# Gate, best and sums for two groups at once, and the chain of scales behind its statistics, in a fused two-layer metaformer kernel

## The reference, cut to what matters

```python
# x: (4, 128, 128, 128) = batch, channels, height, width
x = x + deform_conv(_ln_c(x), w_off, w_conv)             # layer 0, conv
t = _to_tokens(x)                                        # (4, 16384, 128)
t = t + moe(_ln_t(t), router_w, router_b, expert_w, expert_b)   # 8 experts, the best 2 of each token
x = _from_tokens(t, x)
x = x + fourier_conv(_ln_c(x), alphas, betas)            # layer 1, conv: real part is a channel mix and a reversal of the pixels
t = _to_tokens(x)
t = t + soft_moe(_ln_t(t), gate_w, gate_b, weight1, weight2)

def soft_moe(x, ...):                                    # the part that the change touches most
    logits = einsum('bsd,ed->bse', x, gate_w) + gate_b   # 64 experts
    probs = softmax(logits, axis=1)                      # over the 16384 tokens of an image
    vals, idx = top_k(probs.transpose(0, 2, 1), 8)       # the 8 best tokens of each expert
    # gather those tokens, weigh them, two-layer network with gelu, scatter back
```

## Time and profile before

| | before |
|---|---|
| median of 3 runs | 3716.45 us (3716.29 to 3724.53) |
| profiled execution | 3721.06 us |
| span of its instructions | 3719.3 us |
| PE, DVE busy | 3471.8 us (93%), 2835.3 us (76%) |
| ACT, POOL busy | 1759.2 us (47%), 2049.9 us (55%) |
| DVE's wait for `P` (L1231) | 8.2 us in all |
| steady part of `phase_bc` | two steps in 21.9 us |

### The profile page before, as it was taken

The page is one execution under the profiler, slowest core; times in us unless marked ns, Lnnn a source line. Parts: engine busy times, 40 slices in busy tenths (PEclk is TensorE's granted clock), DMA queues, the critical chain, the costliest instruction groups (busy, mean ns, idle before and its releaser), DMA issues. The chain is left out here.

```text
span 3719.3 us, 89516 instructions
## 1 busy us (share of the span) xinstructions
PE 3471.8 (93%) x30679; PEld 2278.8 (61%) x30679; DVE 2835.3 (76%) x8858; ACT 1759.2 (47%) x5333; POOL 2049.9 (55%) x3060
## 2 busy tenths in 40 slices
PE   5999999999999999999987999999999999995668
PEld 4776777777777776777754555555555555553445
DVE  4777777777777767777637999999999999996534
ACT  3444444444444444444411555555555555555234
POOL 4666656666566665666524556665566556654210
PEclk7999999999999999999988999999999999997855
DMA  5555555555555555555526887888788878884689
GB/s 117 130 125 133 125 119 129 125 133 126 118 129 125 132 126 117 126 127 122 113 66 236 295 301 278 292 297 300 280 289 301 295 285 289 312 319 163 241 338 395
DMA packets 665753, 750.30 MB, mean 202 GB/s; under 512 B 104801, under 2 KB 531937, under 8 KB 648914
## 3 DMA queue, kind: packets, MB, share of 16 engines
q1 hardware_dynamic: 559826, 670.61, 58.1%
q10 hardware_dynamic: 104448, 71.85, 6.4%
q0 software_dynamic: 1024, 2.10, 0.2%
HBM read 552.36 MB, written 181.50 MB: 197 GB/s over the span
## 5 line engine op out<-in xcount | busy, mean ns | idle before, releaser
L421 PE MATMUL a_sb<-a_sr,wcv 128*128 128x512 f32 (+3 forms) x2820 | 1052.0, 515 | 0.8 <-DVE a_xo L557 0.8
L403 PEld LDWEIGHTS a_sb<-a_tt,a_win 32*128 32x128 f32 x19008 | 642.9, 187 | 124.2 <-issue 124.0
L421 PEld LDWEIGHTS a_sb<-a_sr,wcv 128*128 128x128 f32 x2820 | 492.9, 190 | 335.0 <-issue 289.9
L403 PE MATMUL a_sb<-a_tt,a_win 32*128 32x144 f32 (+1 forms) x19008 | 661.8, 292 | 25.8 <-ACT a_yr L462 7.4
L1231 DVE TENSOR_TENSOR b_P<-b_P,b_x 128x1024 f32<-128x1024 f32 x512 | 604.1, 1210 | 8.4 <-DMA b_P<-pd 8.2
L480 ACT COPY a_sr<-a_sb 128x432 f32<-128x432 f32 (+14 forms) x1172 | 363.7, 389 | 395.6 <-PE a_sb L403 395.6
L509 DVE COPY a_sr<-a_sb 128x432 f32<-128x432 f32 (+14 forms) x1172 | 419.7, 414 | 137.2 <-PE a_sb L403 127.5
L1121 PE MATMUL b_z<-b_P,b_ew 128*128 128x512 f32 x1024 | 472.6, 604 | 0.0
L435 ACT ACTIVATE a_tn<-a_sb,a_rs 128x128 f32<-128x128 f32 x512 | 192.8, 457 | 582.5 <-POOL a_rs L574 582.5
L1118 PE MATMUL b_z<-b_P,b_ew 128*128 128x512 f32 x1024 | 466.3, 599 | 0.0
L550 DVE STREAM_TRANSPOSE a_tt<-a_sx 128x576 f32<-128x576 f32 x520 | 402.2, 774 | 16.8 <-POOL a_sx L582 8.1
(11 more groups left out here) (188 smaller groups left out, 5348.9 us busy)
## 6 DMA issues: line engine op xcount, KB each, us to landing
b_P<-pd SPq DMA_DIRECT2D x128, 2048.0 KB, 8.7
a_win<-xtp SPq DMA_DIRECT2D x2144, 36.0 KB
a_xin<-in_x SPq DMA_DIRECT2D x128, 256.0 KB, 3.2
xtp<-a_tn ACTq DMA_DIRECT2D x128, 256.0 KB, 4.7
x1d<-a_xo SPq DMA_DIRECT2D x128, 256.0 KB, 4.1
b_x<-x1d SPq DMA_DIRECT2D x128, 256.0 KB
x2d<-b_xa SPq DMA_DIRECT2D x128, 256.0 KB, 3.8
pw<-x3d SPq DMA_DIRECT2D x128, 256.0 KB, 6.6
```

The costliest lines, as they stand in the source:

```text
L403: t = e.matmul(d[:, 0:3 * m_, t0:3, NU_ * i:NU_ * i + nx], win[32 * q:32 * q + 32, half_of(Q, j) % NWH, NWIN // 3 * h + i, :], m, start=(j ...
L421: t = e.matmul(ob[:, r:r + m, :], k["wcv"][:, 3 * (2 - kr) + kx, :], rows[:, :, t_, :], start=(t_ == 0 and r == 0), stop=(t_ == 8))
```

## The change

- `gate`, `best` and `sums` work on two groups at once, in every second step: `gate` in the even steps, 512 pixels of one group to each half of the bank; `best` and `sums` in the odd steps on 512 columns. `lo` and `nm` have two buffers in place of three, the lists half their length, and so have the arrays and the eight searches of `phase_de`.
- `turn_scale` turns the factors of two groups in one matmul, in every second step.
- `rs` has four buffers. The chain of `scales` no longer waits for the products, and only for the router's weights of the pair before: it starts when the step's statistics are done.

```diff
@@ order_b
-            n = NS if stage == "scales" else NG + 3 if stage == "weights" else NG
-            if stage in ("turn_p", "p_out") and (s - lag) % 2 == 0:
+            n = {"scales": NS, "weights": NG + 3, "turn_scale": NG + 1}.get(stage, NG)
+            if stage in ("turn_p", "p_out", "gate", "best", "sums") and (s - lag) % 2 == 0:
+                continue
+            if stage == "turn_scale" and (s - lag) % 2:
                 continue
@@ tensor
-                e.matmul(X[:, 0:4], rev[:, :], rs[:, (G + 7) % 2, 0:4], start=True, stop=True).then_inc(scale_turned, 1)
+                z = (G + 6) % 4
+                e.matmul(X[:, 0:8], rev[:, :], rs[:, z:z + 2, 0:4], start=True, stop=True).then_inc(scale_turned, 1)
...
-                    t = e.matmul(X[64 * j:64 * j + 64, 0:256], gw[:, :], tnT3[:, u, 256 * j:256 * j + 256],
-                                 start=True, stop=True)
+                    t = e.matmul(X[64 * j:64 * j + 64, :], gw[:, :], tnT3[:, j, :], start=True, stop=True)
@@ scalar
-                w.wait_ge(gated, G + 1)
-                w.wait_ge(summed, G - 2)
-                e.activation(lo[:, G % 3, :], X[:, 0:256], ACT.Identity, bias=gb[:, 0:1]).then_inc(x_free, 1)
+                q = G // 2
+                w.wait_ge(gated, q + 1)
+                w.wait_ge(summed, q - 1)
+                e.activation(lo[:, q % 2, :], X[:, :], ACT.Identity, bias=gb[:, 0:1]).then_inc(x_free, 1)
@@ vector
-                e.max(v, lo[:, G % 3, :]).then_inc(top_ready, 1)
-                w.wait_ge(top_ready, G + 1)
-                e.max_index(ci[:, b, 8 * h:8 * h + 8], v, lo[:, G % 3, :]).then_inc(best_ready, 1)
+                e.max(v, lo[:, q % 2, :]).then_inc(top_ready, 1)
+                w.wait_ge(top_ready, q + 1)
+                e.max_index(ci[:, b, 8 * j:8 * j + 8], v, lo[:, q % 2, :]).then_inc(best_ready, 1)
@@ gpsimd
-                w.wait_ge(p_ready, min(G, NG) // 2)
-                w.wait_ge(z_ready, min(G - 3, NG))
+                w.wait_ge(p_ready, (min(G, NG) - 2) // 2)
...
-                w.wait_ge(scale_turned, min(G - 8, NG))
-                w.wait_ge(tn3_ready, min(G - LAG - 2, NG))
-                e.tensor_tensor(rs[:, u, c], ss[:, u, 2, c], k["mhalf"][:, c], ALU.pow).then_inc(scaled, 1)
+                g = min(G - 11, NG - 1)
+                w.wait_ge(scale_turned, (g + g % 2) // 2 + 1 if g >= -1 else 0)
+                w.wait_ge(tn3_ready, min(G - LAG - 4, NG))
+                e.tensor_tensor(rs[:, G % 4, c], ss[:, u, 2, c], k["mhalf"][:, c], ALU.pow).then_inc(scaled, 1)
@@ phase_de
-    pf = S("d_pf", [128, NP_, 8]); cf = S("d_cf", [128, NP_, 16 * GI]); gx = S("d_gx", [128, NP_, 2 * GI])
-    hit = S("d_hit", [128, 2, 16 * GI])
+    pf = S("d_pf", [128, NP_, 8]); cf = S("d_cf", [128, NP_, 8 * GI]); gx = S("d_gx", [128, NP_, GI])
+    hit = S("d_hit", [128, 2, 8 * GI]); eq = S("d_eq", [128, 8, 128])
```

More of the change, by code:

```diff
@@ L1033, in phase_bc @@
     pT = S("b_pT", [128, NPT, 128])
-    xn = S("b_xn", [128, 2, 4, 128]); xa = S("b_xa", [128, 3, 4, 128]); rsr = S("b_rsr", [128, NG, 4])
+    xn = S("b_xn", [128, 2, 4, 128]); xa = S("b_xa", [128, 3, 4, 128]); rsr = S("b_rsr", [128, NG + 2, 4])
     x2r = S("c_x2", [128, 3, 4, 128]); x3t = S("c_x3", [128, 3, 4, 128])
-    tn3 = S("c_tn", [128, 2, 4, 128]); tnT3 = S("c_tnT", [128, 2, 512]); lo = S("c_lo", [128, 3, 256])
-    nm = S("c_nm", [128, 3, 1]); cv = S("c_cv", [128, B, 8 * GI]); ci = S("c_ci", [128, B, 8 * GI], U32)
-    cs = S("c_cs", [128, B, GI])
+    tn3 = S("c_tn", [128, 2, 4, 128]); tnT3 = S("c_tnT", [128, 2, 512]); lo = S("c_lo", [128, 2, 512])
+    nm = S("c_nm", [128, 2, 1]); cv = S("c_cv", [128, B, 4 * GI]); ci = S("c_ci", [128, B, 4 * GI], U32)
+    cs = S("c_cs", [128, B, GI // 2])
     PS = lambda name, shape: ctx.enter_context(nc.psum_tensor(name, shape, F32))
@@ L1171, in scalar @@
             elif stage == "turn_scale":
-                w.wait_ge(scale_turned, G + 1)
-                e.copy(rsr[:, G, :], X[:, 0:4]).then_inc(x_free, 1)
+                w.wait_ge(scale_turned, G // 2 + 1)
+                e.copy(rsr[:, G:G + 2, :].rearrange("p g r -> p (g r)"), X[:, 0:8]).then_inc(x_free, 1)
             elif stage == "turn2":
@@ L1183, in scalar @@
                 w.wait_ge(filtered, G + 1)
-                w.wait_ge(x_free, users["turn_scale", G] + 1)
+                w.wait_ge(x_free, users["turn_scale", G + u] + 1)
                 w.wait_ge(x3_out[G % 3], 16 * moves(G - 3) if G >= 3 else 0)
@@ L1203, in scalar @@
                     f = e.activation(tn3[:, u, r, :], x3t[:, G % 3, r, :], ACT.Copy,
-                                     scale=rs[:, (G + LAG + 1) % 2, 8 + r:9 + r])
+                                     scale=rs[:, (G + LAG + 1) % 4, 8 + r:9 + r])
                 f.then_inc(tn3_ready, 1)
@@ L1207, in scalar @@
                 w.wait_ge(turned3, G + 1)
-                w.wait_ge(gated, G - 1)
+                w.wait_ge(gated, G // 2)
                 e.copy(tnT3[:, u, :], T3[:, :]).then_inc(tnT3_ready, 1)
             elif stage == "gate":
-                w.wait_ge(gated, G + 1)
-                w.wait_ge(summed, G - 2)
-                e.activation(lo[:, G % 3, :], X[:, 0:256], ACT.Identity, bias=gb[:, 0:1]).then_inc(x_free, 1)
+                q = G // 2
+                w.wait_ge(gated, q + 1)
+                w.wait_ge(summed, q - 1)
+                e.activation(lo[:, q % 2, :], X[:, :], ACT.Identity, bias=gb[:, 0:1]).then_inc(x_free, 1)
             elif stage == "sums":
-                b, h = divmod(group_c(G), GI)
-                w.wait_ge(top_ready, G + 1)
[L1217 to L1221, removed]
+                q = G // 2
+                b, j = divmod(q, GI // 2)
+                w.wait_ge(top_ready, q + 1)
+                e.activation(nm[:, q % 2, :], cv[:, b, 8 * j:8 * j + 1], ACT.Copy, scale=-1.0).then_inc(nm_ready, 1)
+                w.wait_ge(nm_ready, q + 1)
+                w.wait_ge(best_ready, q + 1)
+                e.activation(lo[:, q % 2, :], lo[:, q % 2, :], ACT.Exp, bias=nm[:, q % 2, :],
+                             accum_out=cs[:, b, j:j + 1]).then_inc(summed, 1)
     def vector(e):
@@ L1258, in vector @@
                 Z, q = G - 3, G // 2
-                v, n = q % 2, R_STEPS * q + 1
+                v, n, z = q % 2, R_STEPS * q + 1, q % 2 * 2
                 pair = G < NG and G % 2 == 1
@@ L1336, in vector @@
             elif stage == "best":
-                b, h = divmod(group_c(G), GI)
-                v = cv[:, b, 8 * h:8 * h + 8]
+                q = G // 2
+                b, j = divmod(q, GI // 2)
+                v = cv[:, b, 8 * j:8 * j + 8]
                 w.wait_ge(x_free, users["gate", G] + 1)
-                e.max(v, lo[:, G % 3, :]).then_inc(top_ready, 1)
-                w.wait_ge(top_ready, G + 1)
-                e.max_index(ci[:, b, 8 * h:8 * h + 8], v, lo[:, G % 3, :]).then_inc(best_ready, 1)
+                e.max(v, lo[:, q % 2, :]).then_inc(top_ready, 1)
+                w.wait_ge(top_ready, q + 1)
+                e.max_index(ci[:, b, 8 * j:8 * j + 8], v, lo[:, q % 2, :]).then_inc(best_ready, 1)
     def gpsimd(e):
@@ L1432, in sync @@
                 p, a = 64 * (b % 2), b // 2
-                w.wait_ge(best_ready, G + 1)
-                w.wait_ge(summed, G + 1)
+                w.wait_ge(best_ready, G // 2 + 1)
+                w.wait_ge(summed, G // 2 + 1)
                 for q in range(2):
-                    for t, d, n in ((k["cv"], cv, 8 * GI), (k["ci"], ci, 8 * GI), (k["cs"], cs, GI)):
+                    for t, d, n in ((k["cv"], cv, 4 * GI), (k["ci"], ci, 4 * GI), (k["cs"], cs, GI // 2)):
                         e.dma_start(t[p:p + 64, a, q * n:q * n + n], d[64 * q:64 * q + 64, b, :]
@@ L1891, in constants @@
     far = np.zeros((128, 9, 2), np.float32)
-    io = np.zeros((128, 2, 16 * GI), np.float32)
-    i = np.arange(16 * GI)
+    io = np.zeros((128, 2, 8 * GI), np.float32)
+    i = np.arange(8 * GI)
     io[:, 0, :] = i
@@ L1898, in constants @@
             pick[32 * j + b, b // 2, 64 * (b % 2) + j + 60] = 1.0
-    io[:, 1, :] = 512 * (i % (8 * GI) // 8) + 256 * (i // (8 * GI)) + 128
+    pair = i % (4 * GI) // 8
+    io[:, 1, :] = 512 * np.where(i < 4 * GI, GI - 1 - pair, pair) + 128
     far[:, :, 0] = np.arange(9)[None, :] // 3 - 1
```

19 lines of the change are left out of this document (9 added, 10 removed).

## The result

The changed kernel takes 3743.1 us, the median of 8 runs (3731.7 to 3745.6), beside 3719.8 us for 8 runs of the kernel before on the same chips (3715.9 to 3724.5): a ratio of 1.0061, 95% interval 1.0050 to 1.0072. It is slower by 0.6%, where 3688 us and a faster kernel were forecast, and it lies above the range. The profiled execution took 3745.4 us (span 3743.5), 24.2 us more in span than before.

A forecast was written before the change was run, and what follows sets the result against it. The prediction took VectorE with GpSimd's chain as the bound. It summed 59 pairs x 0.43 = 25 us and 4 us in the last block to -29 us, from the 3716.45 us median to 3688, range 3666 to 3722.

The forecast's parts named there:

- How GpSimd gets on beside back-to-back products: Odd group's chain in phase_bc: either slips in between products, stall 0.1 us (taken), or first operation stands, rs 0.8 late.
- It stands behind x3_sum as well: Rival, chance 0.11: the odd chain waits for the products and x3_sum, stall 1.45 us, +0.45 a pair, 3739 us.
- The stall: VectorE's wait for GpSimd's rs at L1265 in each pair: 0.1 us forecast in place of 0.62.
- The spread: Weights' way over the partitions: sent 0.55 us later behind x3_sum, giving back 0.4 us a pair on average.
- The waits for `pd`: Sign in the profile: the product's waits for the spread weights at 20 to 25 us in place of some 8.
- Best's block: VectorE's search over 512 columns in the odd step: 1.41 us in place of twice 0.86, saving 0.31 a pair.
- The gate's slot: TensorE's four gate matmuls of 512 columns: 1.16 us taken, between 0.58 and 1.85.
- The last block: Lists of best values halve after the pairs: 4 us saved, bounds 2 and 6.
- the drain: The pipeline's end, some 15 short steps with fewer but longer links: 0, give or take 2 us.
- TensorE's need: TensorE's time for a pair without gaps: 21.14 us after the change, 21.8 by the upper price of the gate matmuls.
- the case without a spread stall: Rival, chance 0.10: TensorE or SP runs ahead, so the weights' spread costs nothing; -0.75 us a pair, 3666 us.
- Products behind GpSimd: VectorE's products held by GpSimd's powers: nothing booked; as rival, chance 0.06, +1.1 us a pair, 3777 us.

The follow-up runs named there:

- after_gap: The changed kernel with a one-column VectorE memset behind each of the first three of an odd step's four products: 3724.3 us, ratio 1.0025 to the kernel before.
- best_even: The changed kernel with best and sums one step later, so best stands in the even step between the four products and x3_sum: 3666.0 us, ratio 0.9857.
- run 61: Not a label of a run: the words say that 61 products started inside a power in the run of the changed kernel, which takes 3743.1 us.
- after_pout: The changed kernel with the weights' issue (p_out) ahead of load2 in SP's queue: 3725.2 us, ratio 1.0022 to the kernel before.

## Why the prediction was wrong

**The step that failed** is "How GpSimd gets on beside back-to-back products", where I took the first of two ends: the chain slips in at one operation for each product, stall 0.1. In the steady stretch nothing slips in: the chain's first operation stands 5.04 us, and the stall is 1.11 us. The rival named for it, "It stands behind x3_sum as well", is what happened, with 3739 us beside the measured 3743. That its number is so near is luck: it has a stall 0.34 us too large (20 us in 59 pairs) and no wait for the spread (15.5 us more than before), and its +0.45 a pair should be +0.52 by its own terms (1.45 - 0.62 - 0.31). The evidence for the choice was one stretch of the pipeline's filling, where moreover the chain had begun ahead of the products, against a row of the steady stretch (L1381); I gave the first little more weight, and the price of the steady stretch was the right one. The trace of before even had the rival's case, in the one odd step where best had not yet begun and x3_sum follows the products at once:

```profile
2061.80 4.74 POOL L1381 TENSOR_TENSOR b_pp<-b_ss,b_rs 128x4 f32<-128x4 f32 x1
...
2065.78 0.69 DVE L1329 TENSOR_TENSOR c_x<-c_x 128x512 f32<-128x512 f32 x1
```

L1381 ends at 2066.54, behind x3_sum's 2066.47, and not at the products' end at 2065.87. The prediction doesn't use this row. The cause is shown by the runs: the hold is 5.04 us with x3_sum behind the products, 4.44 with mixed or best behind them, and one product long with a memset between. The kernel before had best between the products and x3_sum, which both let GpSimd in and covered 0.86 us of its chain; moving all of best to the odd step took both.

**The stall** was 1.11 us, not the rival's 1.45, and not 0.1. The rival added 0.67 for x3_sum to a chain in which 0.3 for x3_sum's interference was already counted; with the operation held behind it, x3_sum disturbs nothing further. 1.45 less 0.3 is 1.15.

**The spread** was the right loop with too small a price. The issue came 0.5 us later as forecast (in the median pair 3.10 for 2.58, load2 at 2.07 behind L1314's end for 1.55). But from L1314's end to the landing it takes 14.35 us in a pair against 13.17 before, 1.2 and not 0.55: the weights go out 0.4 us later on average (3.10 for 2.73), the issue of the spread comes another 0.2 behind them, and the landing itself takes 8.2 against 7.6, which the prediction had only among what could make it fail. This error was hidden behind the first. With the chain freed alone (`after_gap`) the kernel takes 3724 us, no faster than the kernel before, so the forecast of 3688 would have failed on this term as well. The memsets themselves are some 4 of those 36 us (0.07 us a pair, 59 pairs).

**The sum,** with the measured terms: stalls for `rs` +24.9 us (64.3 less 39.4), waits for the spread +15.5 (23.7 less 8.2), best 59 x 0.31 = -18.3, together +22.1; the pairs took 21.8 more.

**What held.** The waits for `pd` were forecast at 20 to 25 us and are 23.7, though by luck: VectorE came later than forecast, which makes them shorter, and the spread landed later, which makes them longer. Best's block takes 1.40 us (2502.82 to 2504.22) for 1.41 forecast. The gate's slot is 1.01 us (2516.24 to 2517.25) for 1.16. The last block gained 2.9 us for 4; the drain lost 3.8 where 0 give or take 2 was booked. TensorE's need of 21.14 us was too high, since `best_even` turns a pair in 21.02 and has TensorE idle for 1.2% of it; that made the case without a spread stall (3666) look like the floor; `best_even` came to the same number by another way.

**Products behind GpSimd** was rightly booked at nothing. In the changed kernel a product started 0.83 us into a power (2521.52, 2522.35) and took 1.22 us as ever. The Trainium skill ("SBUF — State Buffer", section "SBUF: two separate sides") says that the port pair is held by whoever comes first, for the whole instruction, and that VectorE counts when it has two SBUF inputs or runs in a two-port mode. The part on the inputs agrees with all runs here (x3_sum holds, mixed and MAX8 don't); no run here is about the mode. The part on who comes first agrees for GpSimd behind a product and not for a product behind GpSimd: the power reads SBUF and came first, and by the rule the product would have stood 1.4 us, to 2523.79. In the run 61 products started inside a power, with up to 2.2 us of it left; none of them took more than 1.24 us, and none of all 512 more than 1.303. The profile calls its spans on GpSimd rough, so when a power has its port isn't known.

**What stays open.** While the stage filled, the same operation in the same place passed after one product's length in three cases of four (at 2040.63 as at 2022.05), and was held once; and once in the drain it passed again. GpSimd's timeline of the changed kernel:

```profile
1982.08 1.11 POOL L1365 TENSOR_TENSOR b_ss<-b_st 128x8 f32<-128x8 f32 x1 [0.64 <-DVE b_st L1258]
...
2003.10 4.45 POOL L1365 TENSOR_TENSOR b_ss<-b_st 128x8 f32<-128x8 f32 x1 [2.08 <-DVE b_st L1328]
...
2022.05 1.04 POOL L1365 TENSOR_TENSOR b_ss<-b_st 128x8 f32<-128x8 f32 x1 [2.12 <-DVE b_st L1328]
...
3367.11 1.01 POOL L1365 TENSOR_TENSOR b_ss<-b_st 128x12 f32<-128x12 f32 x1
```

It started 0.17, 0.23, 0.24 and 0.29 us after the first of four products. The second and third have the same offset and the same 8 columns and part all the same, and the last passed with the 12 columns with which it was held in each pair of the steady stretch; so neither offset nor size decides. In `after_pout` and `best_even` it passed in all four cases of the fill. I don't know what lets it pass: the hold through all the products is shown for the steady stretch, not as a rule. Why the spread takes longer to land when it is issued earlier (9.4 to 9.8 us in the three kernels with the weights' issue first) was not isolated either: the issues around it in SP's queue differ as well. Nor was it tested which engine bounds `best_even`.

## What to carry to other kernels

When an instruction is moved, ask what it separated. Here, between VectorE's instructions with two SBUF inputs, one with a single such input was where a small GpSimd instruction got through, and its time was room for GpSimd's chain. Of the same merge, best in the odd step made the kernel 0.6% slower and best in the even step 1.4% faster. Take the price of a disputed meeting from the steady stretch, not from the fill, but look in the fill for orders of instructions that the change will make regular. Idle times too short to be listed as waits add up, too: 0.16 us in each pair were the whole difference of two kernels. And price the second loop with the range of its transfer's landing times, since it shows only once the first is cured.

## What the runs showed of the hardware

- In the steady stretch, a GpSimd operation of 0.21 us that reads SBUF takes 5.04 us behind four back-to-back products and x3_sum, 4.44 behind the products alone, and 1.03 to 1.20 with a memset of one column (0.06 us) behind each of the first three. There the hold is not given up between two of VectorE's instructions that both read two SBUF tiles; in the fill and the drain it sometimes is (1.01 to 1.19 us).
- With three memsets between them, and GpSimd's operations passing, four products and the way to the next instruction take VectorE 4.60 us in place of 4.53: the gaps cost 0.07 us together.
- A product that starts while GpSimd's power runs takes no longer: 61 such products, at most 1.24 us.
- Four gate matmuls of 512 columns, two in each half of the array, take 1.01 us of TensorE's time where four of 256 columns took 0.58.
- With the weights sent out 2.4 us sooner behind L1314 (0.73 for 3.10), the spread landed only 0.9 us sooner (13.44 for 14.35): its own way from issue to landing grew from 8.2 to 9.75 us.
